# A twelve-stage kernel: new instruction orders in the stacks and the decaying stage, written-out last bodies, a deeper flow in two small feed-forward stages

## What is computed

```
# level 1, feed-forward (twice):
real = x @ cos(theta + theta_noise);  imag = x @ sin(phi + phi_noise)
y = sqrt(real * real + imag * imag)
# level 1, attention: an RWKV-6 layer. Per head, over t:
S = exp(-exp(w_t)) * S + k_t^T v_t ;  y_t = r_t @ (S + u * k_t^T v_t)
# level 2, feed-forward (twice): a stack of DEPTH = 6 layers, of width 128
for i in range(DEPTH):
    x = attn_layer(shift_tokens(x), Wqkv[i], q_scale[i], k_scale[i], Wo[i]) + x   # 16 heads of 64, windows of 32
    x = ffn_layer(shift_tokens(x), ln_g[i], ln_b[i], W1[i], b1[i], W2[i], b2[i]) + x
# each block: x = x + 0.5 * block(_layernorm(x))   (1.0 for attention)
```

## Time and profile before

| | |
|---|---|
| median of 3 runs | 5288.11 us (5274.58 to 5289.39) |
| the profiled execution | 5288.43 us, span of its instructions 5286.7 us, mean granted TensorE clock 0.953 |
| first small feed-forward stage | 728.1 to 770.5 us |
| decaying stage | 770.5 to 942.5 us |
| second small feed-forward stage | 942.5 to 985.1 us |
| first stack, with its entry | 985.6 to 2735.3 us |
| second stack, its entry | from 2959 us |
| busy over the span | PE 93%, DVE 73%, ACT 65%, POOL 54% |

### The profile page before, as it was taken

One profiled execution on the slowest core, in us unless ns is written; L12 is line 12 of the kernel. 1 busy time (PEld: TensorE's weight loads), 2 busy tenths in 40 slices (PEclk: granted clock), 3 DMA queues, 4 the chain that ended last, 5 costly groups with the idle time before them and its releaser, 6 DMA issues. The chain is left out here.

```text
span 5286.7 us, 141627 instructions
## 1 busy us (share of the span) xinstructions
PE 4936.9 (93%) x48916; PEld 3439.4 (65%) x48916; DVE 3860.5 (73%) x7094; ACT 3437.7 (65%) x5879; POOL 2869.3 (54%) x3451
## 2 busy tenths in 40 slices
PE   8989968499999999999969699999999999989899
PEld 5656645267777777777746367777777777756656
DVE  2274236488888888888856488888888888845655
ACT  3343323278888888888846388888888888842652
POOL 0010015388788878788830388778787778720200
PEclk9988978699999999999979799999999999989999
DMA  1000000111121111112100111111111112110000
GB/s 44 1 6 34 1 8 2 40 40 50 52 56 51 51 52 52 50 52 56 38 21 1 41 41 55 50 52 52 55 47 56 46 52 56 38 41 1 8 25 9
DMA packets 110452, 195.56 MB, mean 37 GB/s; under 512 B 21408, under 2 KB 28848, under 8 KB 110256
## 3 DMA queue, kind: packets, MB, share of 16 engines
q1 hardware_dynamic: 110256, 192.89, 13.0%
HBM read 53.36 MB, written 1.05 MB: 10 GB/s over the span
## 5 line engine op out<-in xcount | busy, mean ns | idle before, releaser
L2965 POOL TENSOR_TENSOR stage_qk<-stage_halves 128x1024 f32<-128x1024 f32 x384 | 906.3, 2360 | 53.2 <-DVE stage_halves L3081 45.7
L3001 POOL TENSOR_TENSOR stage_qk<-stage_qk,stage_rnorm 128x1024 f32<-128x1024 f32 x384 | 731.0, 1904 | 30.4 <-issue 0.3
L2994 POOL TENSOR_TENSOR stage_probs<-stage_probs,stage_rsum 128x768 f32<-128x768 f32 x384 | 565.4, 1472 | 217.8 <-DVE stage_rsum L3110 205.3
L3078 DVE TENSOR_TENSOR stage_halves<-stage_wide,stage_tables 128x1024 f32<-128x1024 f32 x384 | 468.6, 1220 | 223.2 <-ACT stage_square L2784 183.6
L2784 ACT ACTIVATE stage_square<-stage_wide 128x1024 f32<-128x1024 f32 x384 | 394.0, 1026 | 192.5 <-PE stage_wide L2550 192.1
L3081 DVE TENSOR_TENSOR stage_halves<-stage_wide,stage_tables 128x512 f32<-128x512 f32 x768 | 491.1, 681 | 0.0
L2616 PE MATMUL stage_pv<-stage_probsT,stage_v_win 96*64 96x64 f32 x12288 | 488.2, 227 | 2.7 <-ACT stage_ctxT L2837 1.6
L3090 DVE TENSOR_REDUCE stage_norm<-stage_square 128x16 f32<-128x1024 f32 x384 | 464.9, 1211 | 32.3 <-issue 32.1
L2616 PEld LDWEIGHTS stage_pv<-stage_probsT,stage_v_win 96*64 96x64 f32 x12288 | 408.5, 137 | 122.8 <-issue 98.6
L2567 PE MATMUL stage_turn<-ident,stage_qk 128*128 128x128 f32 x3072 | 479.1, 279 | 4.9 <-ACT stage_qkT L2804 4.7
L2602 PEld LDWEIGHTS stage_flip<-ident,stage_probs 128*96 128x96 f32 x3072 | 355.7, 126 | 192.5 <-issue 129.5
(11 more groups left out here) (302 smaller groups left out, 9898.0 us busy)
## 6 DMA issues: line engine op xcount, KB each, us to landing
stage_v_win<-stage_v SPq DMA_DIRECT2D x384, 192.0 KB, 2.5
stage_v_win<-stage_v SPq DMA_DIRECT2D x384, 128.0 KB, 2.4
stage_v_win<-stage_v SPq DMA_DIRECT2D x192, 64.0 KB, 2.2
stage_wq<-in_T_wq SPq DMA_DIRECT2D x12, 512.0 KB, 4.1
stage_wk<-in_T_wk SPq DMA_DIRECT2D x12, 512.0 KB, 4.9
stage_wv<-in_T_wv SPq DMA_DIRECT2D x12, 512.0 KB, 3.5
stage_wo<-in_T_wo SPq DMA_DIRECT2D x12, 512.0 KB, 3.5
stage_w_up<-in_L_w_up SPq DMA_DIRECT2D x8, 512.0 KB, 7.1
```

The lines of the kernel that those rows point to most:

```text
L2965: nc.gpsimd.tensor_tensor(qk[:, n, :], halves[:, n % 2, 0, :], halves[:, n % 2, 1, :], ALU.add)\
L2994: nc.gpsimd.tensor_tensor(probs[:, m % 2], probs[:, m % 2], rsum[:, m % 2].to_broadcast([P, 2, 2 * HALVES, REACH]), ALU.mult)\
L3001: nc.gpsimd.tensor_tensor(heads, heads, rnorm[:, n, :].rearrange("p (h o) -> p h o", o=1).to_broadcast([P, LH, LD]), ALU.mult).then_inc(at ...
L3078: nc.vector.tensor_tensor(out[:, 0], heads, cos.to_broadcast([P, LH, LD]), ALU.mult)
```

## The change

**Small feed-forward stage.** `xn`, `xT` and `squares` get room for all tiles, the transposes 3 PSUM tiles and the products 4. DVE adds squares of group step-2, ACT takes each root at once, three groups behind (with scale 0.25, which makes the half), under one table preloaded at the start, and POOL adds the root to x.

```diff
+    TURNS, WAVES = 3, 4
-            def add_root(step):
-                dve.wait_ge(*sig("root", step, 1))
-                x = chip.x[:, of(step), :]
-                nc.vector.scalar_tensor_tensor(x, norm2[:, of(step), :], 0.5, x, ALU.mult, ALU.add).then_inc(sig["x"], 1)
...
             statistics(0)
-            for step in range(L1_GROUPS + 1):
...
+            statistics(1)
+            for step in range(L1_GROUPS + 2):
+                if runs(step):
                     normalize(step)
+                if runs(step + 2):
+                    statistics(step + 2)
+                if runs(step - 2):
+                    add_squares(step - 2)
...
+            nc.scalar.preload_act_table_set("sqrt_and_others")
+            for step in range(L1_GROUPS + 3):
+                if runs(step):
                     copy_xT(step)
+                if runs(step - 1):
                     square(step - 1)
+                if runs(step - 3):
+                    root(step - 3)
...
+            def add_root(step):
+                pool.wait_ge(*sig("root", step, 1))
+                nc.gpsimd.tensor_tensor(chip.x[:, of(step), :], norm2[:, of(step), :], chip.x[:, of(step), :], ALU.add).then_inc(sig["x"], 1)
```

```diff
-            for s in range(-2, B + 2):
+            for s in range(-2, B + 4):
                 body(s)
...
-            nc.gpsimd.memset(weights[:, :, :, :, :], 0.0).then_inc(once["set"], 1)
...
+                if s == -3:
+                    nc.gpsimd.memset(weights[:, :, :, :, :], 0.0).then_inc(once["set"], 1)
```

```diff
-                nc.gpsimd.memset(v_win[:, :, :, :], 1.0).then_inc(once["set"], 1)
+                nc.gpsimd.memset(v_win[0:WINDOW, 0, :, :], 0.0).then_inc(once["set"], 1)
...
+                nc.scalar.preload_act_table_set("natural_log_exp_and_others")
...
-                for layer in range(DEPTH):
-                    table(layer)
-                dve.wait_ge(*once("tables", 1))
+                table(0)
+                dve.wait_ge(*once("tables", 0, 1))
...
+            for layer in range(1, DEPTH):
+                nc.gpsimd.tensor_tensor(tables[:, layer], base[:, :, :, :], rows[:, layer].to_broadcast([P, 4, HALVES, LD]), ALU.mult)\
+                  .then_inc(once["tables"], 1)
```

```diff
-        straight = qk[:, 2, :].rearrange("p (a s) -> p a s", s=SEQ)
+        straight = square[:, 0, :].rearrange("p (a s) -> p a s", s=SEQ)
...
+            def turn_out(b):
+                if b == 0:
+                    pe.wait_ge(*att("v", STEPS - 1, HALVES))
+                pe.wait_ge(att["leave"], att.base["leave"] + b + 1)
+                if b > 1:
+                    pe.wait_ge(att["left"], att.base["left"] + b - 1)
+                for t in range(HALVES):
+                    ins = nc.tensor.transpose(wide[:, b % 2, t * P:(t + 1) * P], straight[:, b % 4, t * P:(t + 1) * P], chip.ident[:, :])
+                ins.then_inc(att["tok"], 1)
...
-            for s in range(STEPS - 2, STEPS + 2):
-                body(s)
-            for b in range(B):
...
+            tail()
```

1172 lines of the change are left out of this document (752 added, 420 removed).

## The result

The kernel after takes 5199.78 us (median of 4 runs, 5197.44 to 5201.32) against 5288.75 for the kernel before in the same session. The ratio is 0.9827, with a 95% interval of 0.9813 to 0.9841. Forecast were 5214, between 5180 and 5246. The total is near and the sign is right, but the terms of the sum are not: one has the wrong sign, one came to a quarter of what the runs show. So the terms are what this part is about.

A forecast was written before the change was run, and what follows sets the result against it. It took PE's own stream to bound the stack loop, at 34.44 us a step, and handover chains the other stretches. Terms 32 + 10 + 11 + 9 + 12 = 74 off 5288.4 gave 5214 us, range 5180 to 5246.

The forecast's parts named there:

- Small stages: Two small feed-forward stages: waiting two groups back with own buffers cuts a group from 5.06 to 2.35 us, 32 us gained.
- The lock: Small stages: DVE and POOL exclude each other on a shared port, 2.5 us a group, ending about 1 us later.
- Decaying stage: New order brings the intervals between batches from 15.50 towards PE's 12.76 us; 10 us gained, between 20 gained and 8 lost.
- Loop: Stack loop: new order saves 0.1 us in each of 92 steps, 9 us, between 23 gained and 5 lost.
- the ring: Loop: q or k chunks through `wide` (product, square, turn) follow every 5.61 us; tightest margin said to widen, 0.11 to 0.26.
- The trade of pairs and borders: Loop: six `weigh` runs become five, saving 0.15 us a step, against changed group-size borders; taken as 0.1 a step.
- Entry: Stack entry: shorter memset stall, five tables off DVE and an earlier table load gain 5.5 us each, 11 for both.
- Fill: Stack fill, up to the first `output`: no net change once the stack's end is counted, 0 within 3 us.
- the shift in phase: Stack: `output` begins about 2.8 us later in the fill and is ahead by as much at the end.
- Ends: Stack ends: quicker way back of the batches (2.9) and written-out order (3) gain 6 us each, 12 for both.
- The third rival: Loop: ACT's copy of v waits for the values' window transfers; 7 in 100 slower than before, 6 more for a stall.
- The first rival: Small stages gain only 18 us as DVE and POOL block each other, decaying stage 0: 5238 us, 12 in 100.

The follow-up runs named there:

- e1: The changed kernel's small feed-forward stage alone put into the kernel before: 5253.99 us against 5291.37, ratio 0.9937.
- e2: The new order of the decaying stage alone put into the kernel before: 5286.19 us, ratio 0.9998.
- e9: Kernel after with DVE's update 2 of the queries moved ahead of normalize_y in the decaying stage: 5180.08 us, ratio to before 0.9796.
- e7: Kernel before with ACT squaring only the first 512 of 1024 columns of each q and k chunk: 5252.18 us in one run.
- e4: Kernel before with the stack's entry alone changed (five tables on POOL, small memset, early table load): 5293.08 us against 5291.37, ratio 1.0005.
- e5: Kernel after without the written-out last bodies, the 8 batches going back one after the other behind them: 5207.09 us, ratio 0.9852.

## Why the prediction was right in sum and wrong in parts

- **Small stages, 32 forecast, 37.7 measured (37 in e1).** The mechanism is right in the main: the chain of handovers no longer sets the period. The term was put at 2.35 us a group. From the first squares added (7.18 us into the stage, forecast 7.2) to the last (21.00) it is 1.97, since the statistics of five groups are done before the first squares come. The lock that the prediction weighed is there (0.96 for 0.42, 1.00 for 0.60) and costs 1.5 us in the first stage, but the prediction left out that DVE would stand another 2.0 us for a power that POOL's list has behind an addition. With the additions on DVE both are gone, and the same distance is 1.65 a group. The end, put at 1.9, takes 2.95, POOL's four additions one after the other, and 1.95 with them on DVE.
- **Decaying stage, 10 forecast, 3 lost in the profiles, nothing in the timed e2.** The step that failed is what it drew from this: "POOL's addition of x to the mixes now has a `weigh`, a turn and two levels of other batches on PE between the mix and its first reader." The sentence is true, and PE hardly waits for it (0.9 us). But it looked at who waits for the addition, and not at who can't run beside it: the new DVE list puts update 2 there, and PE waits for that, 1.6 us a batch. It also took PE's busy time as given, where that rose from 128.8 to 134.6 at a lower clock. The Trainium skill, "SBUF — State Buffer", section "Who interferes with whom", says that a DVE instruction with two SBUF inputs contends with a GpSimd instruction that reads SBUF, and that one with at most one SBUF input does not, outside the modes in which DVE uses two ports. The trace agrees on both, 2.18 us for the update and 1.09 for normalize_y, which reads PSUM, beside the same addition. One SBUF input alone doesn't make an instruction safe: the normalization of the small stage has one tensor input in SBUF, and takes 1.00 for 0.60 beside POOL. The prediction used the rule for the small stages and not here. Without the stall the forecast would have been about right, 158.7 in e9, 12.8 under before; but 4.0 of these are PE's busy time, for which the forecast has no more than "some more with the clock", so this is in part luck.
- **Loop, 9 forecast, 36 measured.** The step that failed: "PE never stood. So the new tightest margin, 0.26, is wider than the old, 0.11." (By its own numbers the new margin is 5.9 - 5.61 = 0.29.) The old distance was not PE's own time but the ring's, 5.71 and in the second stack 5.80; PE's own was 5.56 (e7), under the 5.61 of the ring, so the old margin was below zero. A sign of it stood in the earlier trace rows: the prediction gave the 1.98 us of the projection at 1837.90 to a small-tile group in front of it, but that one stands behind transpositions, and e7 has 1.88 there. This wait is 0.26 of the 0.33 us saved per step in the first stack and 0.35 of the 0.53 in the second. The trade of pairs and borders, put at 0.1, leaves 0.07. In the second stack the distance 3-4 was longer by 0.12 in before, and half squares didn't change it. Of it 0.09 lie in the row of `output`, 3.72 us against 3.63, whose first product takes 0.32 in place of 0.23, as a held one would; what holds it stays open, and after has no such difference.
- **Entry, 11 forecast.** It was right to 0.4 us each at the first projection, and e4 shows that it is worth nothing in the old kernel, since the fill gives most of it back. The step that failed is the tacit one, that what starts sooner ends sooner. **Fill, 0 within 3:** 9.1 us more than the shift in phase; with the entry alone, e4, the fills grow by 7.1.
- **Ends, 12 forecast:** 10.0 by e5 for the part meant, and 11.5 for the new order, where the shift in phase was put at 5.6.
- **The third rival** was real and harmless. ACT does stand for the transfers of the values' window, in all 43 steps:

```profile
L2928 ACT ACTIVATE stage_v<-stage_wide 128x1024 f32<-128x1024 f32 x86 | 88.1, 1025 | 85.2 <-DMA stage_v_win<-stage_v 67.0 <-PE stage_wide L2550 18.2
```

That is 67.0 / 43 = 1.56 us a step, under the 2 us that `output` covers, and PE has no wait at all in that stretch. The first rival, at 18 us for the small stages, took the lock for more than it costs and had the decaying stage nearly right. That the sum landed near the forecast is in good part luck: the loop's error, +27, and the decaying stage's, -13, and the fill's, -9, partly cancel.

## What to carry to other kernels

When an order moves a long POOL instruction that reads SBUF, look at what DVE runs at that moment, not only at who waits for POOL: put instructions there that kept their time beside POOL here, as normalize_y from PSUM and the statistics did, and take the critical ones that read two tensors in SBUF out of its way. Look also at what POOL's own list now has behind the new instruction. A PE row that is busy all the time doesn't prove that PE is the bound: compare the distance of the starts around a shared buffer with the ring of that buffer, and shorten the ring once. A gain in front of a stretch with a low clock has to be measured at the end of that stretch, and a stage at a low clock is to be split into busy and idle time before its length is put down to a wait.

## What the runs showed of the hardware

- A float32 projection of 4 x 512 columns holds PE for 1.72 us when it stands behind a group of transpositions and for 1.82 behind small-tile groups, or when it was held; the first of a pair of value groups costs 0.61, the second 0.46 or 0.47.
- Waits of PE that made a distance 0.15 and 0.24 us longer left no idle time in the profile; with the 0.10 in the held products 0.26 and 0.35 us a step were hidden so, over 43 steps measured in each stack.
- A DVE multiplication and a subtraction of two SBUF tensors beside a POOL addition that started first ended 0.14 to 0.3 us behind it: 2.18 and 2.06 us in place of 0.28 and 0.41. Beside the same addition a DVE instruction that reads PSUM kept its 1.09.
- PE's busy time for the same 2192 instructions of the decaying stage ranged from 134.6 us at a granted clock of 0.72 to 117.2 at 0.81, and with the same code from 128.8 at 0.75 to 122.3 at 0.80. Stages with unchanged code at a clock below 1.00 differed between executions by up to 9 us (decaying stage, old order) and 13 us (the attention between the stacks, 223.2 to 236.2); 43 steps of the loop at 1.00 differed by 0.1 us at most.
